# Moving the copy of a finished context out of PSUM from VectorE to ScalarE in a macaron MoE / latent-attention / MoE kernel

## The reference, cut to what matters

```
latents = x @ W_down.T
keys    = latents @ W_uk.T ;  values = latents @ W_uv.T
q       = x @ W_q.T                       (16 heads of 128)
scores  = q . k / sqrt(128), causal mask
attn    = softmax(scores)
ctx     = attn . v
out     = ctx @ W_o.T
```

## Time and profile before

| | |
|---|---|
| median of three timed runs | 251.86 us (251.26 to 251.86) |
| the profiled execution, device time | 251.87 us |
| its span, first to last instruction | 249.9 us |
| busy: PE / PEld / DVE / ACT / POOL | 237.5 / 182.1 / 206.2 / 163.6 / 71.9 us |
| granted TensorE clock | 1.000 over the span |
| line 765, the copy: 30 instructions | 11.8 us, 394 ns each |
| line 764, the reciprocal: 30 instructions | 5.2 us, 173 ns each |

### The profile page before, as it was taken

The page is one execution under the profiler, slowest core; times in us unless marked ns, Lnnn a source line. Parts: engine busy times, 40 slices in busy tenths (PEclk is TensorE's granted clock), DMA queues, the critical chain, the costliest instruction groups (busy, mean ns, idle before and its releaser), DMA issues.

```text
span 249.9 us, 7272 instructions
## 1 busy us (share of the span) xinstructions
PE 237.5 (95%) x2643; PEld 182.1 (73%) x2668; DVE 206.2 (82%) x487; ACT 163.6 (65%) x320; POOL 71.9 (29%) x127
## 2 busy tenths in 40 slices
PE   7789999999789999999999999999998899999995
PEld 2545479966667868879788787787887788855474
DVE  2978799895879989999999899999999518268793
ACT  2646581485878887978888798888889500335560
POOL 8320234000003434524354334344455000210230
PEclk9999999999999999999999999999999999999999
DMA  6999400001102014216034160251427330000005
GB/s 223 236 312 352 89 4 0 3 0 45 42 3 67 21 31 95 43 46 122 10 76 81 42 125 1 70 100 32 96 41 87 24 63 3 0 0 3 0 1 168
DMA packets 34792, 17.21 MB, mean 69 GB/s; under 512 B 25484, under 2 KB 34520, under 8 KB 34520
## 3 DMA queue, kind: packets, MB, share of 16 engines
q1 hardware_dynamic: 33576, 15.81, 27.6%
q10 hardware_dynamic: 1200, 1.18, 1.4%
HBM read 7.55 MB, written 1.05 MB: 34 GB/s over the span
## 4 chain that ended last, share of the span: by engine, by line
PE 77%; DVE 16%; issue 3%; DMA 1%; ACT 1%; DVEq 0%
PE bank L1088 12%; PE bank L901 10%; PE bank L852 9%; PE bank L1163 8%; PE bank L1079 7%; PE bank L1008 6%; PE bank L1078 4%; PE bank L1102 3%; PE bank L1101 3%; PE bank L1103 3%; PE bank L1035 3%; PE bank L1080 2%; DVE pT_lo L756 2%; DVE nmax L751 2%; DVE nmax L747 2%
## 5 line engine op out<-in xcount | busy, mean ns | idle before, releaser
L506 ACT ACTIVATE prob<-bank,nmax 128x384 f32<-128x384 f32 (+3 forms) x128 | 62.3, 528 | 8.2 <-DVE nmax L747 6.8
L756 DVE TENSOR_TENSOR pT_lo<-bank,pT_hi 128x512 f16<-128x512 f32 x80 | 54.6, 684 | 3.1 <-ACT pT_hi L512 2.4
L512 ACT CAST pT_hi<-bank 128x512 f16<-128x512 f32 x80 | 46.8, 585 | 11.1 <-PE bank L1088 10.6
L1088 PE MATMUL bank<-ident,prob 128*128 128x128 f32 x320 | 50.5, 280 | 0.2 <-ACT prob L506 0.2
L387 POOL TENSOR_TENSOR cst<-craw,rsum 128x256 f32<-128x256 f32 x30 | 18.4, 614 | 93.2 <-DVE craw L765 93.2
L1101 PE MATMUL bank<-lat,pT_hi 128*128 128x65 bf16 x320 | 37.7, 193 | 2.3 <-DVE pT_lo L756 2.3
L1102 PE MATMUL bank<-lat,pT_hi 128*128 128x64 bf16 x320 | 37.8, 195 | 0.0
L1079 PE MATMUL bank<-latT_lo,wqo 128*128 128x384 bf16 (+3 forms) x128 | 36.6, 299 | 1.2
L1103 PE MATMUL bank<-lat,pT_lo 128*128 128x65 bf16 x320 | 37.5, 192 | 0.0
L1101 PEld LDWEIGHTS bank<-lat,pT_hi 128*128 128x128 f16 x320 | 30.1, 96 | 7.2 <-DVE pT_lo L756 2.0
L747 DVE TENSOR_REDUCE nmax<-bank 128x1 f32<-128x512 f32 (+1 forms) x48 | 32.8, 682 | 2.1 <-PE bank L1080 2.1
(11 more groups left out here) (173 smaller groups left out, 463.5 us busy)
## 6 DMA issues: line engine op xcount, KB each, us to landing
wqo<-stage SPq DMA_DIRECT2D x64, 64.0 KB, 2.0
wqo<-in_L_attn_W_q_dram SPq DMA_DIRECT2D x1, 2048.0 KB, 9.5
wqo<-in_L_attn_W_o_dram SPq DMA_DIRECT2D x1, 2048.0 KB, 15.6
out_dram<-X SPq DMA_DIRECT2D x8, 128.0 KB, 1.8
X<-in_L_attn_x_dram ACTq DMA_DIRECT2D x1, 512.0 KB, 7.1
cT<-in_L_attn_W_uk_dram SPq DMA_DIRECT2D x1, 512.0 KB, 11.2
cT<-in_L_attn_W_uv_dram SPq DMA_DIRECT2D x1, 512.0 KB, 11.0
cT<-in_L_ffn_w_dram SPq DMA_DIRECT2D x1, 384.0 KB, 4.8
```

The source lines that it names most:

```text
L506: last = nc.scalar.activation(prob[:, u % 2, cols], bank[SCORE_BANK[u]][:, cols], ACT.Exp, bias=nmax[:, u, n:n + 1])
L512: nc.scalar.copy(pT_hi[:, j % 2, :], bank[3 + j % 2][:, :]).then_inc(pThi_ready, 1)
L756: nc.vector.tensor_tensor(pT_lo[:, j % 2, :], bank[3 + j % 2][:, :], pT_hi[:, j % 2, :], ALU.subtract).then_inc(pTlo_ready, 1)
L1088: last = nc.tensor.transpose(bank[3 + j % 2][:, blk(k)], prob[:, j % 2, blk(k)], ident[:, :])
```

## The change

`take_context` is divided. DVE keeps the waits and the reciprocal (renamed `invert_sums`). The copy goes to ACT's step, behind `exponent` and ahead of the queries' split and of `split`. On ACT it waits for the buffer `craw` (`clo_ready`), for the context (`ctx_ps`), and also for DVE's reciprocal of the same context (`rsum_ready`), and it now raises `ctx_free`. Nothing else is changed: the 30 copies are of the same shape, and `normalise_last` stays.

```diff
+            def take_context(i, side, b):          # ACT
+                src = bank[5 + b][:, 0:SB * (LAT + 1)].rearrange("p (q l) -> p q l", q=SB)
+                act.wait_ge(clo_ready, i * (2 * B) + (side * B + 1 + b))
+                act.wait_ge(ctx_ps, i * (2 * B) + (side * B + b + 1))
+                act.wait_ge(rsum_ready, i * (2 * B) + (side * B + b + 1))
+                nc.scalar.copy(craw[:, b, :, :], src[:, :, 0:LAT]).then_inc(ctx_free, 1)
             def attention_step(i, j, queries=True):    # ACT
+                side, unit = divmod(j - 1, HU)
                 if not beyond(i, j + 3):
                     exponent(i, j + 3)
+                if j and unit in LAST_UNIT:
+                    take_context(i, side, LAST_UNIT.index(unit))
                 if queries and j in (1, 3):
                     split_queries(i + 1, j // 2)
                 if not beyond(i, j + 2):
...
-            def take_context(i, side, b):          # DVE
+            def invert_sums(i, side, b):
                 src = bank[5 + b][:, 0:SB * (LAT + 1)].rearrange("p (q l) -> p q l", q=SB)
                 dve.wait_ge(clo_ready, i * (2 * B) + (side * B + 1 + b))
                 dve.wait_ge(ctx_ps, i * (2 * B) + (side * B + b + 1))
                 nc.vector.reciprocal(rsum[:, b, :], src[:, :, LAT]).then_inc(rsum_ready, 1)
-                nc.vector.tensor_copy(craw[:, b, :, :], src[:, :, 0:LAT]).then_inc(ctx_free, 1)
...
-                    take_context(i, side, LAST_UNIT.index(unit))
+                    invert_sums(i, side, LAST_UNIT.index(unit))
                 if not beyond(i, j + 1):
                     split(i, j + 1)
```

## The result

The kernel with the change took 252.50, 255.82, 255.18 and 253.58 us, a median of 254.38; the kernel before took 251.86 (251.26 to 252.23) beside it. The ratio is 1.0095 [1.0061, 1.0128]: slower, above the forecast's own range (251.9 to 252.6) and above the wider one (251.2 to 253.5). Two later series on other chips gave 252.70 against 251.97 and 252.62 against 251.82, ratios of 1.0033 [1.0014, 1.0053] and 1.0037 [1.0016, 1.0057]: just above the own range and inside the wider one. So there are two things to explain: 0.7 to 0.8 us that is always there, and more in three of the first four executions, whose granted TensorE clock was 0.993, 0.987 and 0.993 where that of the first, the profiled one, was 1.000. This first one took 252.50, with a span of 250.7 (before: 251.87 and 249.9), so its trace shows the first part alone.

A forecast was written before the change was run, and what follows sets the result against it. The first seven passes were taken as bound by PE with DVE right behind, the eighth by DVE. 0 in seven passes and +0.33 in the eighth on 251.87 gave 252.2 us, own range 251.9 to 252.6, wider 251.2 to 253.5.

The forecast's parts named there:

- The removal: DVE loses 30 copies of 394 ns, 1.24 us of queue a pass; by itself worth nothing in the first seven passes.
- The copy on ACT: 30 copies out of PSUM behind ACT's exponentials, each holding its queue 0.28 us, 0.39 at most, with no wait holding.
- Context 7 can start at 131.28: Step 5 of a pass: low part of unit 7 at 130.54 plus 0.74; PE arrives at 131.29, margin 0.01 us.
- Context 10: Step 8 of a pass: low part at 134.63, context can start at 135.37; PE arrives at 135.39, margin 0.02 us.
- The passes' sum: First seven passes: contexts 7 and 10 hold, the other copies cost nothing; 0 us added.
- The eighth pass: Late high parts outweigh DVE's gain; context 9 goes from 196.20 to 196.53, 0.33 us later.
- the first one: Rival: the copies make ACT the second bound in every pass; 252.6 to 253.9 us, chance 0.37.
- The shorter eighth pass: Rival: ACT absorbs the copies and waits ahead of contexts 6 and 7 go; at or below 251.1 us, chance 0.11.

The follow-up runs named there:

- the removal alone: From the kernel before: DVE copies one column of each block, 135 ns in place of 394, and ACT copies nothing; 251.56 us, ratio 0.9990.
- the moved wait: Changed kernel with PE's wait for the freed bank at the head of its step, ahead of queries and scores; 252.23 us, ratio 1.0016.
- two kernels with still longer ones: Changed kernel with each ACT copy made twice, 257.17 us; changed kernel with idle ACT copies ahead of high parts 7 and 9 of the eighth pass, 254.68 us.
- the two kernels with the copy behind the high part: Changed kernel with ACT's copy behind the high part: 251.47 us, ratio 0.9975; the same plus PE's bank wait at the step's head: 251.02 us, ratio 0.9963.
- the passes only: Changed kernel with the 28 copies of the first seven passes on ACT, the eighth pass's two on DVE; 252.60 us, ratio 1.0019.
- the eighth pass only: Changed kernel with only the eighth pass's two copies on ACT, the other 28 on DVE; 252.11 us, ratio 1.0018.
- the addition alone: From the kernel before: DVE keeps its copies and ACT makes a second one that nobody reads, in the change's place; 252.69 us, ratio 1.0023.

## Why the prediction was wrong

Its mechanism was right and one margin was wrong; a second cost it did not price at all.

- **The removal.** Forecast: worth nothing in the passes, something in the eighth. Shown by the removal alone: six passes shorter by 0.13 in all, 0.10 of it in the first, and 0.56 us in sum.
- **The copy on ACT.** Forecast 0.37 to 0.40 us directly behind an exponential, without a wait, and 0.28 of the queue. It took 373 ns, waited for nothing and held the queue 0.25, below the 0.27 under which nothing was to come out; the high part behind it ran 0.61 in place of 0.59. From the exponentials to the low part of unit 7 the forecast had 130.54 - 128.91 = 1.63, the trace 1.62.
- **The step that failed: "Context 7 can start at 131.28. PE gets to it at 131.29. It holds by 0.01 us."** It used 0.74 from the start of a low part to its context, a value from a context behind one wait. Context 7 waits twice, and took 0.83. A nearer row was there: context 7 of the eighth pass follows its low part by 193.80 - 192.98 = 0.82. With 0.82 the sum gives 131.36, 0.07 late, which is what happened. The experiment with the moved wait shows it: with the scores between the two waits it is 0.75, and the loss of the passes is gone; where the two waits stayed together, in step 7 of the eighth pass, it is still 0.83.
- **Context 10, "It holds by 0.02 us".** It held, but by luck: it has two waits as well. Its low part started 12.74 behind context 1 (134.80), so by 0.83 it was ready at 13.57, and PE, itself late by context 7, came at 13.60. Had PE been on the time of before, 13.53, this margin would have failed too: with the moved wait PE was on that time, and the low part started 12.74 behind context 1 as well.
- **The passes' sum.** Forecast 0; measured 0.38 over six passes in the first profile, nearly all in five of them, since the first pass took 16.30 before as well. Other profiles of kernels with the copy ahead of the high part had 0.03 to 0.05 a pass more, between context 0 and context 1 of the next pass; that stays open.
- **The eighth pass.** Forecast +0.33 from the seventh pass's last copies on; measured +0.43 - 0.06 = +0.37. The path up to the low part of unit 17, unit 7 of this pass, came as forecast: it starts 193.74 - 185.90 = 7.84 behind context 1, against 192.98 - 185.55 = 7.43 before, 0.41 later, and 193.39 - 192.98 = 0.41 was forecast. From there the sum took the same 0.74; with the 0.82 that its own rows show, it gives 0.41 for the contexts, and context 9 came 0.43 later behind context 1. The waits ahead of contexts 6 and 7 were not to shrink in sum: 0.79 became 0.97. Where the copy alone is on ACT in the eighth pass it was +0.15.
- **The rivals.** What came true is the first one's sign ("PE waits for low parts", passes of 16.3) by another mechanism: not a copy that holds ACT longer, for it held it less, but a consumer that starts later. Its price was the lower end, 252.6 to 252.7 in the two repeats. The shorter eighth pass failed for the reason given, and came true once the copy stood behind the high part.
- **What was not priced.** Falls of the granted clock took the first median to 254.38: taken off as 1 - clock of each span, an estimate of 3.3, 1.8 and 1.8 us, they leave 252.5, 253.4 and 251.8, where later executions of the change at full clock took 251.88 to 254.25. The prediction costed PE's longer waits in the eighth pass as waits alone (0.27 to 0.75, 0.63 to 0.89). In the profiles of two kernels with still longer ones the clock fell directly behind such waits, with shortfalls of 1.7 and 3.4 us. For the change itself no execution with a lower clock was profiled, so that its falls lie in the same place is argued from these. In all, executions at 0.994 or below were 5 of 90 for the kernel before, 5 of 28 for the change, none of 36 for the two kernels with the copy behind the high part and the removal alone; none in 36 and 5 in 90 are too close to call different. With the moved wait, the passes only, the eighth pass only and the addition alone it was one in each. What makes the clock fall is open, and so is why three of the first four fell, and later two of 24.

## What to carry to other kernels

Work moved onto an engine with spare time still has a place in its queue: ahead of an instruction with two followers in series it delays them all, and one line later it cost nothing and let the whole gain of the removal through. When a forecast holds by hundredths of a microsecond, take each hand-over from a row of the same consumer with the same waits ahead of it. And look for a lost hand-over in the length of a pass and in the idle time of the weight loads, since an engine whose ends are modelled can look fully busy.

## What the runs showed of the hardware

- In the passes context 7 started 0.83 us behind its low part's start with two waits directly ahead of it, and 0.75 with one of them moved ahead of the scores; in the eighth pass, where no scores stood between, it stayed at 0.83.
- In two profiled executions the granted clock fell to 0.50, its lower level, within a microsecond of a context that PE had waited for: behind waits of 1.03 and 0.88 us in one, behind one of 1.58 in the other. The shortfalls were 1.7 and 3.4 us, and other executions of the same two programs kept their clock.
- Behind a 373 ns copy out of PSUM the next instruction of ACT started after 0.25 us, an overlap of 0.12.
